# 64x64 tiles in place of 32x32 tiles for the skip products of a Fourier-layer tower, and a token stage with unread matmuls between its products

## The reference, cut to what matters

```python
def _fourier_layer(v, W1, W2):
    x_ft = jnp.fft.rfft2(v)              # 12 + 12 by 12 modes are kept
    ...
    return jnp.fft.irfft2(out_ft, s=(Sx, Sy))
for i in range(L):                       # L = 4, v: 64 images, 32 channels, 64 x 64
    x1 = _fourier_layer(v, W1, W2)
    x2 = jnp.einsum('bcxy,cd->bdxy', v, w_w[i]) + w_b[i][None, :, None, None]
    v = x1 + x2
    mean = jnp.mean(v, axis=(0, 2, 3), keepdims=True)
    var = jnp.var(v, axis=(0, 2, 3), keepdims=True)
    v = (v - mean) * jax.lax.rsqrt(var + BN_EPS)
    v = v * bn_g[i][None, :, None, None] + bn_b[i][None, :, None, None]
    if i < L - 1:
        v = jax.nn.relu(v)
...
# token stage: h is [64, 65, 64]
h = h + _L0_attn_ref(_layernorm(h, axis=-1), ...)
h = h + _L0_ffn_ref(_layernorm(h, axis=-1), ...)
```

## Time and profile before

| what | before |
|---|---|
| median of 3 executions (lowest, highest) | 1347.76 us (1342.45, 1348.53) |
| the profiled execution's own time | 1344.41 us |
| its span, first to last instruction | 1342.4 us |
| PE, DVE, ACT, POOL busy | 1164.1, 849.5, 555.0, 373.2 us |
| mean granted TensorE clock | 0.936 of full |
| DMA | 300.29 MB, mean 224 GB/s |

### The profile page before, as it was taken

One profiled execution on the slowest core, in us unless ns is written; L12 is line 12 of the kernel. 1 busy time (PEld: TensorE's weight loads), 2 busy tenths in 40 slices (PEclk: granted clock), 3 DMA queues, 4 the chain that ended last, 5 costly groups with the idle time before them and its releaser, 6 DMA issues.

```text
span 1342.4 us, 40668 instructions
## 1 busy us (share of the span) xinstructions
PE 1164.1 (87%) x18235; PEld 665.2 (50%) x18235; DVE 849.5 (63%) x1044; ACT 555.0 (41%) x811; POOL 373.2 (28%) x536
## 2 busy tenths in 40 slices
PE   5898899999989899898998989999889886964696
PEld 4554555555544455454555445555555552324652
DVE  7575676777757567576775756666666571048664
ACT  2165354444546344344444644444434471111150
POOL 8672113224244304031333530222212351110000
PEclk8899899999999999899999998999899988885788
DMA  6578999998328999999963889999998177841001
GB/s 166 142 201 214 273 245 227 216 236 200 98 90 222 234 333 362 345 351 322 343 199 92 202 234 342 349 328 366 321 308 248 29 269 250 352 168 38 1 1 32
DMA packets 156119, 300.29 MB, mean 224 GB/s; under 512 B 33064, under 2 KB 100024, under 8 KB 139012
## 3 DMA queue, kind: packets, MB, share of 16 engines
q1 hardware_dynamic: 131656, 251.53, 61.1%
q0 software_dynamic: 20864, 44.73, 11.9%
q10 hardware_dynamic: 3426, 1.44, 0.4%
HBM read 147.86 MB, written 128.48 MB: 206 GB/s over the span
## 4 chain that ended last, share of the span: by engine, by line
PE 61%; DVE 11%; DMA 10%; ACT 6%; issue 6%; SPq 5%; POOL 1%; DVEq 0%; ACTq 0%; POOLq 0%
PE ps L1647 14%; PE ps L1686 12%; PE ps L1721 7%; PE ps L1709 7%; PE ps L1609 4%; PE ps L1672 3%; PE ps L1573 3%; DMA arena<-maps 3%; DMA maps<-arena 2%; SPq L1171 2%; PE ps L1786 2%; ACT arena L1450 1%; PE ps L1548 1%; PE ps L1588 1%; DMA half_inverse<-arena 1%
## 5 line engine op out<-in xcount | busy, mean ns | idle before, releaser
L1686 PEld LDWEIGHTS ps<-arena 48*128 48x128 f32 x3072 | 187.7, 194 | 91.9 <-issue 86.4
L1686 PE MATMUL ps<-arena 48*128 48x128 f32 x3072 | 207.8, 286 | 12.0 <-issue 6.4
L1450 ACT ACTIVATE arena<-ps,arena 128x1024 f32<-128x1024 f32 x96 | 112.3, 1202 | 225.3 <-PE ps L1686 199.9
L1120 POOL DMA_DIRECT2D arena<-arena x207 | 120.4, 589 | 293.8 <-ACT arena L1467 289.9
L1459 ACT ACTIVATE ps<-ps 128x1024 f32<-128x1024 f32 x144 | 145.5, 1011 | 102.6 <-PE ps L1647 102.5
L2104 DVE STREAM_TRANSPOSE arena<-ps 128x1024 f32<-128x1024 f32 x96 | 177.5, 1932 | 1.2 <-PE ps L1709 1.2
L1647 PE MATMUL ps<-arena 32*32 32x512 f32 x2944 | 152.1, 610 | 10.9 <-DMA arena<-maps 7.5
L2091 DVE STREAM_TRANSPOSE arena<-arena 128x2048 f32<-128x2048 f32 x64 | 144.3, 2289 | 20.6 <-issue 14.2
L1709 PE MATMUL ps<-arena 32*32 32x512 f32 x3072 | 149.8, 604 | 4.6 <-DVE arena L2091 3.4
L1721 PE MATMUL ps<-arena 128*64 128x96 f32 x2304 | 124.5, 260 | 31.3 <-DVE arena L2104 25.7
L1721 PEld LDWEIGHTS ps<-arena 128*64 128x64 f32 x2304 | 105.4, 144 | 81.4 <-issue 45.5
(11 more groups left out here) (321 smaller groups left out, 1438.7 us busy)
## 6 DMA issues: line engine op xcount, KB each, us to landing
arena<-half_inverse SPq DMA_DIRECT2D x90, 384.0 KB, 11.6
half_inverse<-arena SPq DMA_DIRECT2D x120, 256.0 KB, 4.5
maps<-arena SPq DMA_DIRECT2D x112, 256.0 KB, 4.5
maps<-inputs SPq DMA_DIRECT2D x112, 256.0 KB, 12.0
arena<-maps SPq DMA_DIRECT2D x28, 1024.0 KB, 17.4
maps<-arena SPq DMA_DIRECT2D x28, 1024.0 KB, 15.3
inputs<-maps SPq DMA_DIRECT2D x28, 1024.0 KB, 20.6
arena<-in_mode_w POOLq DMA_DIRECT2D x48, 384.0 KB, 7.4
```

The source lines that it names most:

```text
L1120: eng.dma_start(dst, src).then_inc((modes_st[batch % 2], last_st, late_st)[part], 16)
L1450: nc.scalar.activation(half(h_out(l, q), h)[:, 1024 * pair:1024 * pair + 1024], ps[:, 2 * pair:2 * pair + 2, :].rearrange("p b n -> p (b n ...
L1686: last = nc.tensor.matmul(ps[:, b, at:at + 128], gtile[s][rows, 4 * b + 2 * h + n, :], iy[rows, :], start=False, stop=(i >= 2 and n == 1))
```

## The change

**Passes.** `blocks64` takes the place of `blocks32` in both sets: for each pair of banks four products of 64x64 weights (the block-diagonal weights of two images, with zeros between them) by 512 columns: two row halves r by two column halves x. The records of a set of two pairs fall from 32 to 16. So that pair 0 holds what the first pair of `blocks64` needs, banks 0 to 3 now hold column blocks 0, 2, 1, 3 (`columns_of`); ACT and DVE write each pair of banks to two blocks that stand apart (`of_pair`). The map's layout in HBM changes, and each half map is stored by two transfers from 64 partitions in place of four from 32, with runs of 4 KB in place of 2 KB.

**Token stage.** 33 unread products (`keep_warm` with bank 3) stand between the products; one square of 128x1024 moves from DVE to ACT; the splitting of w1 and the router moves on DVE ahead of `masked(J_KV2)`, and the second half of the first `last_norm` (now `scaled`) behind it.

```diff
@@ token stage, ACT
+            act.wait_ge(ln_sum, 3 * len(NORMED) + 1)
+            nc.scalar.activation(sq[:, 0:1024], dev[:, 0:1024], ACT.Square).then_inc(ln_root, 1)
             last_root(0, 0, 16)
@@ token stage, PE (SPARE = 3)
             key_values(J_KVC, groups[2])
+            keep_warm(SPARE, 7)
             for i, (turned_to, products, k) in enumerate(((J_N1T, J_KV, J_ATT), (J_N1T2, J_KV2, J_ATT2))):
                 pe.wait_ge(n1_ready, i + 2)
                 turn_sides(turned_to, groups[i])
+                keep_warm(SPARE, (4, 7)[i])
                 pe.wait_ge(kv_ready, i + 2)
                 key_values(products, groups[i])
+                keep_warm(SPARE, 2)
                 begin(k)
...
                 last.then_inc(job_full[k % 2], 1)
+                if i == 0:
+                    keep_warm(SPARE, 7)
...
+                if i == 0:
+                    keep_warm(SPARE, 4)
             wait_evacuated(pe, J_N2T2)
@@ token stage, DVE
             attended(J_ATT, 0)
-            last_norm(0, 0, 16)
-            masked(J_KV2, 1024)
+            centred(0, 16).then_inc(ln_sum, 1)
             dve.wait_ge(tok_in, 16 * LATE)
             for whole, high, low in ((w1, w1h, w1l), (router, rth, rtl)):
...
+            masked(J_KV2, 1024)
+            dve.wait_ge(ln_root, 3 * len(NORMED) + 1)
+            scaled(0, 0, 16)
             attended(J_ATT2, 1024)
@@ passes
+        def columns_of(b):
+
+            return 2 * (b % 2) + b // 2
+
+        def of_pair(tile, pair):
+
+            return tile.rearrange("p (r y n) -> p y r n", r=2, y=2)[:, pair]
@@ passes, SP: map_store
-                    blocks = dst.rearrange("(g c) (j n) -> j c g n", g=4, j=QUAD)
-                    for j in range(QUAD):
-                        src = half(h_out(l, i), h)[32 * j:32 * j + 32].rearrange("c (g n) -> c g n", g=4)
+                    blocks = dst.rearrange("(g p) (j n) -> j p g n", g=2, j=2)
+                    for j in range(2):
+                        src = half(h_out(l, i), h)[64 * j:64 * j + 64].rearrange("p (g n) -> p g n", g=2)
                         sp.dma_start(blocks[j], src).then_inc(map_st[i % 2], 16)
@@ passes, PE
-            def blocks32(w, source, h, pair, last_one):
-                for x in range(4):
-                    for r in (2 * pair, 2 * pair + 1):
-                        rows = slice(32 * r, 32 * r + 32)
-                        at = 2048 * h + 512 * x
-                        last = nc.tensor.matmul(ps[32 * x:32 * x + 32, r, :], w[rows, 32 * r:32 * r + 32],
+            def blocks64(w, source, h, pair, last_one):
+
+                for x in range(2):
+                    for r in range(2):
+                        rows = slice(64 * r, 64 * r + 64)
+                        at = 2048 * h + 1024 * x + 512 * pair
+                        last = nc.tensor.matmul(ps[64 * x:64 * x + 64, 2 * pair + r, :], w[rows, rows],
                                                 source[rows, at:at + 512], start=True, stop=last_one)
                 return last
```

53 lines of the change are left out of this document (29 added, 24 removed).

## The result

| what | after | beside it, before |
|---|---|---|
| median of 4 executions each (lowest, highest) | 1332.84 us (1328.72, 1337.65) | 1348.14 us (1342.45, 1354.42) |
| ratio, 95% interval | 0.9893 [0.9848, 0.9939] | |
| the profiled execution's own time, its span | 1328.72, 1326.9 us | 1344.41, 1342.4 us |

The account below looks back on a forecast made before the run. TensorE's order was taken to bound pass 0, TensorE and transfers each part of passes 1 and 2. Pass 0 4.8, passes 1 and 2 11, issue -2, token stage 5 made +19 on 1344.4: 1363, as median 1366 us, range 1347 to 1388.

Parts of the forecast that it names:

- Pass 0: TensorE's order sets the pace; the longer 64x64 set of half 0 adds 0.30 us in each of 16 quads, +4.8 us.
- The tile changes: Switches between 32x32 and 64x64 tiles in the passes, 0.10 us each: hidden, costed at nothing; 12 us without cover.
- clean term: Longer 64x64 sets in passes 1 and 2 where TensorE sets the pace: 32 x 0.30 + 12.6 = +22.2 us.
- the idle: Passes 1 and 2 idle 32 us more than pass 0, in waits for transfers; this hides half the added time, leaving +11.
- issue at -2: TensorE's idle ending in "issue" ahead of L1647, 3.0 us in one of two groups; half the instructions save 2 us.
- Token stage: After the passes: unread products delay DVE, reordering wins some back; +9.0 + 0.2 - 2.7 - 1.4 = +5, between -1 and +14 us.
- They do not: In the token stage, 64x64 products get no faster once the clock is up; L517, L525 and L545 stay at 3.68 us.
- rival (b): Token stage: small products double their pace at full clock, first delay 5.3 instead of 9.0, stage about 0; 1361 us, chance 0.10.
- -2.7 and -1.4: Token-stage gains: DVE's chain from L763 to L545 shortens by 2.7 us; the first L576 falls from 5.12 to 3.71, -1.4.
- (d): Queue on SP: half as many store issues let loads behind them start earlier, faster; 1333 us if half of 94 goes, chance 0.12.
- (a): Passes 1 and 2: nothing is absorbed, they give all 22 us; +32 in total, 1380 us, chance 0.18.
- (c): Transfers set passes 1 and 2 throughout, passes hide all, token stage near -1 to +3; 1350 us, no change, chance 0.13.

Follow-up runs that it names:

- token_only: The kernel before with only the token stage of the change, its passes, layout and stores as before: 1349.04 us, ratio 0.9993 to before.
- fewer_warm: The changed kernel with three and one unread products ahead of the first group's transposes and keys by values, instead of seven and four: 1327.08 us, ratio 0.9831 to before.
- next64_cold: The kernel before with 64x64 next sets and the changed token stage, without unread products ahead of the first keys by values: 1331.66 us, 0.985 of before.
- split64: The changed kernel with each 64x64 product of 512 columns cut into two of 256: 1351.62 us, ratio 1.0077 to before.

## Why the prediction was wrong

**Pass 0: right.** One quad of pass 0 after, in the order of the earlier trace rows:

```profile
207.63 1.96 PE L1674 MATMUL ps<-arena 64*64 64x512 f32 x16
...
209.64 1.30 DVE L2102 BATCH_NORM_STATS2 arena<-ps 128x6 f32<-128x512 f32 x2 [0.72 <-PE ps L1674]
...
214.60 1.21 PE L1748 MATMUL ps<-arena 128*64 128x96 f32 x24 [0.49 <-DVE arena L2131]
215.74 1.95 PE L1674 MATMUL ps<-arena 64*64 64x512 f32 x16
...
217.91 1.02 ACT L1485 ACTIVATE ps<-ps 128x1024 f32<-128x1024 f32 x1
218.76 1.46 PE L1699 MATMUL ps<-inputs,arena 32*128 32x512 f32 x8
```

The set is 1.96 us long (I said 1.96), DVE starts 2.01 after it (2.07), the out set no longer waits for ACT (1.46 in place of 1.93; I said 1.53). The quad's median period went from 15.30 to 15.57, +0.27 for +0.30, and the pass +4.2 for +4.8 (over all kernels the pass 0 of before took 258.4 to 259.1 us, but 261.9 in token_only, and with 64x64 next sets of whole products it took 261.8 to 263.4). The tile changes are hidden, as costed; the Trainium skill's drain at a change of tiling mode (TensorEngine Tiling (Array Packing), Key Properties), priced at 12 us if none were hidden, doesn't show in the pass.

**Passes 1 and 2, clean term: right in kind.** Where transfers are out of the way and the 10.3 us of issue are taken off, the 32x32 kernel needs 529.7 - 10.3 = 519.4 us and the 64x64 kernel 537.7: +18.3, where I had +22.2.

**Passes 1 and 2, the idle: the step that failed.** I wrote "They idle more than pass 0 does", took the 32 us for transfers, let half of the clean term hide in it, and costed issue at -2 "for both". Of the 562.1 us before, 519.4 are clean and 42.7 are not: 22.0 issue, 7.5 maps and 13.2 of neither. Of the 546.8 after, 537.7 are clean and 9.1 not: 0, 6.0 and 3.1. So +18.3 - 22.0 - 1.5 - 10.1 = -15.3, where I had +9. The idle wasn't slack that a longer set could use; it came with the many instructions of the short sets and went with them. That is the step that failed. The 10.1 I put down to the clock, from rows and without a kernel of its own for it. Two windows of before around the gap at 945, granted clock in the last but two columns:

```profile
936.00:943.00 7.00, 7.00 (x160) 3.84 (x160) 3.12 (x4) 2.68 (x5) 5.71 (x10) 1.00 1.02 340
947.00:953.00 6.00, 4.92 (x47) 4.53 (x47) 2.26 (x2) 2.30 (x2) 0.00 (x0) 0.50 1.03 323
```

It is at 2.4 GHz ahead of the stand of 2.98 us, and at 1.2 GHz after it. The same holds behind the gaps at 824.8 and 998.0 (0.51 and 0.50), and behind a wait of 4.49 us for a map at 540 (0.50 over 10 us): 30.6 us at 1.2 GHz behind these four in the trace's clock records, which at half the pace can cost 15 us at most; after has none of them in its passes, and both kernels have some 3 us more at the end of each pass. Not every gap does it: behind the 2.83 us at 610.6 and the 1.64 at 910.9 the clock stays at 1.00.

**Token stage: +5 predicted, -1.1 measured.** TensorE and DVE from the first unread product on:

```profile
1189.65 7.70 PE L493 MATMUL ps<-arena 128*128 128x512 f32 x14
...
1197.29 2.08 PE L520 MATMUL ps<-arena 64*64 64x64 f32 x64
1199.30 3.70 PE L493 MATMUL ps<-arena 128*128 128x512 f32 x8
1202.93 2.08 PE L528 MATMUL ps<-arena 64*64 64x64 f32 x64
...
1205.06 1.22 DVE L755 TENSOR_TENSOR arena<-ps,arena 128x1024 f32<-128x1024 f32 x1 [8.43 <-PE ps L528]
...
1247.47 3.71 PE L584 MATMUL ps<-arena 128*64 128x128 f32 x64 [1.99 <-DVE arena L819]
```

The unread products took 7.64 us for 8.9, and 3.63 for 3.6. But the 64x64 products by 64 columns take 2.08 us at full clock, not 3.68: "They do not" was wrong, and rival (b) right. I had carried it over from L1573 with four tiles at once, 1.59 and 1.55 us at the two levels, to L520 and L528 with two, with no row for that. The wait of DVE grew by 4.5 us, not 9.0: 1.3 less for the first seven, 1.6 for each of two small sets. The trace has 3.68 / 2.08 = 1.77 for two tiles and 1.03 for four. For one record that is 57.5 and 32.5 ns on two tiles, and 33.1 and 32.3 on four (1.59 and 1.55 over 48): only the two tiles at 1.2 GHz were above the 32 to 33 ns at which the others stand. The Trainium skill, TensorE: Matmul & The Clock Gate, Part 1, has the start-to-start time as the columns over the clock, and some 2.5 ns more once the array is warm. An estimate from that for 64 columns is 53 and 29 ns, a factor of 1.8; the trace agrees for two tiles and not for four. The second L584 came down to 3.71 as said. The rest of the chain gained what the -2.7 and -1.4 promised and 1.5 more, as far as one profile can tell. Over all kernels a stage change of 1 us isn't clear of noise; that the 5 us longer stage didn't come is.

With three and one unread products (fewer_warm) DVE's wait is about that of before, 3.24 us for 3.92, and with none (next64_cold) 3.43, where L520 ran at the lower clock and L528 for most of its length:

```profile
1189.86 5.09 PE L493 MATMUL ps<-arena 128*128 128x512 f32 x6
...
1200.08 1.22 DVE L755 TENSOR_TENSOR arena<-ps,arena 128x1024 f32<-128x1024 f32 x1 [3.24 <-PE ps L528]
```

```profile
1198.43 3.68 PE L520 MATMUL ps<-arena 64*64 64x64 f32 x64 [0.19 <-ACT inputs L442]
1205.36 3.19 PE L528 MATMUL ps<-arena 64*64 64x64 f32 x64 [3.25 <-DVEq L761]
...
1208.58 1.23 DVE L755 TENSOR_TENSOR arena<-ps,arena 128x1024 f32<-128x1024 f32 x1 [3.43 <-PE ps L528]
```

Stages of 132.7 and 132.2 us: the early ones are worth nothing, and eleven of them cost 5 us. The gain of 6 to 7 us on the 139.0 of before is in what stands behind: the order of DVE, the square on ACT, and the later unread products, which no run separates.

**The rivals.** (d) named the right sign and time (1333) for the wrong reason, by luck: stores and queue order gain nothing. It priced arrivals and queues off the chain by line, where lateness of instructions doesn't stand out. Of (a), (b) and (c), (b) was right on its own point and worth some 5 us.

**What stays open.** Why the idle grows so fast above 32 records a us, and why it isn't gone at a DMA share of 0.50: what sets when the next packet is asked for isn't in the trace. Why split64 has a third of the idle of before with as many records: its pace is a little lower (34.4 for 35.8), and its sets take 2.04 us for as many records as the 32x32 sets get through in 1.51, but no run separates the two. Two of 63 executions of before took 1320.3 and 1328.7 us, so the time isn't fixed by the program; whether their idle was smaller isn't known, since neither was the profiled one. The last mix up to the token stage took 127.1 to 133.6 us over the kernels, in no order of their changes; the 3.3 us that after gained there I can't assign to the change. And passes 1 and 2 of kernels with the same passes differ by 5 us (542.1 to 547.6), by maps that come late or don't. split64 keeps its 7 us.

## What to carry to other kernels

Add up the idle class "issue" of an engine over all its lines, stage by stage, before costing anything; if it stops inside a run of instructions that has no wait, look at when its instruction packets land. Work on few, large instructions can then be faster than the same work on small ones that the array does sooner: here 20 us more of busy time went with 36 us less of idle. And don't let an edit hide in idle time until it is clear what makes that idle; it may be the very thing that is edited, and a loop made shorter again waits for the next bound (here the maps, 22.5 us).
